# Recurrent two-tower kernel: output sizes folded into the combine weights, high part cast on VectorE, groups half a stage apart

## The chip, the cores and the metric

The kernel runs on one core of a Trainium2 chip. The metric is the device time of one execution in microseconds (us), the median of several runs. The engines named below are TensorE (PE in the profile; its weight loads are PEld), VectorE (DVE), ScalarE (ACT), GpSimd (POOL) and SyncE (SP, which here only issues transfers).

## What is computed

The reference scans 128 steps. At each step a batch of 512 rows with 12 features goes through two small residual towers, and the step's result `delta` replaces feature 3 of the next step. The path tower does not see `delta`; the flat tower does, so only the flat tower and the head form a chain from step to step.

```python
def _leaky(x):
    return jnp.where(x >= 0, x, NEG * x)          # NEG = 0.2
def _tower(x, w_in, b_in, blocks):
    h = _leaky(x @ w_in + b_in)
    for w1, b1, w2, b2 in blocks:                  # two blocks
        h = _leaky(_leaky(h @ w1 + b1) @ w2 + b2 + h)
    return h
def step(prev_delta, xk):
    fk, k = xk                                     # fk: 512 x 12
    d = jnp.where(k == 0, fk[:, DELTA_IDX], prev_delta)
    fk = fk.at[:, DELTA_IDX].set(d)                # DELTA_IDX = 3
    fe = _tower(fk[:, :4], fw_in, fb_in, flat_blocks)
    pe = _tower(fk[:, 4:], pw_in, pb_in, path_blocks)
    h = _leaky(jnp.concatenate([fe, pe], axis=-1) @ cw1 + cb1)
    delta = jax.nn.sigmoid(h @ cw2 + cb2)[:, 0]
    return (delta, delta)
```

All hidden widths are 128, all data float32.

## The kernel before

Hidden units lie on the 128 partitions and the batch on the columns. The flat tower and the head work on two **groups** of 256 columns (g = 0 and 1). The path tower works on all 512 columns, with its products split in two halves (h = 0 and 1). One **stage** is one step k of the scan; in the stage of step k the path tower works ahead, on steps k+1, k+2 and k+3.

**Products.** A float32 product (`product`, L438; `onto`, L441; `combine_path`, L528; `combine_flat`, L533) is one matmul call on 256 columns and shows as two matmul instructions in the profile. A stage has 20 of them: 8 of the path tower, 8 of the flat tower (`flat_1a`, `flat_1b`, `flat_2a`, `flat_2b` for two groups), 4 of the head's combine layer. Seven calls per stage work on split operands of the type fp32r and show as one instruction each: `path_in` (512 columns, L453), `flat_x` (256 columns, one per group, L497), `output_high` (L541) and `output_low` (L546), one each per group. For the last two the head activation is split into a high part rounded to fp32r (`head_hi`) and a remainder (`head_lo`). They multiply with `cw2_sign`, a matrix of +1 and -1, because the sizes |cw2| are already in the head activation: ScalarE computes leaky(|cw2|*x + |cw2|*cb1), with `cw2_size` as its scale and `cb1_scaled` as its bias.

**Order of work.** Each engine has a list of calls written by hand, `body(k)`, run for k = -3 to 127; an engine runs its own list strictly in order, and semaphores tie the lists together. So the place of a call in its engine's list decides when it can run at the earliest. Between the products of a group ScalarE computes an activation: `flat_1a` on TensorE, `flat_1a` on ScalarE (tile `f_mid`), `flat_1b` on TensorE, `flat_1b` on ScalarE (`f_res`), and the same again for block 2, then `combine_flat`, `head_out` and `head_high` on ScalarE, `head_low` on VectorE, the two output products, `delta_out` on ScalarE (sigmoid), then `flat_delta` and `flat_in` on VectorE (`f_t`, `f_in`) for the next step. VectorE also adds the residual input to the result bank ahead of the second product of a block (`flat_1b_old`, `flat_2b_old`), and makes the path tower's sums and results (`path_1b_sum`, `path_1b`, `path_2b_sum`, `path_2b`; tiles `p_sum`, `p_res`). ScalarE makes `p_in` and `p_mid`.

TensorE's list before is `body` at L549, ScalarE's at L300, VectorE's at L417.

**Set-up.** SyncE loads the features in four chunks; VectorE (chunk 0) and GpSimd (chunks 1 to 3) split them into a high and a low part, which are stored to memory and loaded again per step (`x_flat`, `x_path`). The weights `hidden_w` are one transfer. Before its list TensorE waits for the weights and for `cw2_sign` and `cb1_scaled` (`s_cw2`), and opens the two result banks with one product each.

## Time and profile before

| | |
|---|---|
| median of 3 runs | 1308.1 us (1307.48 to 1308.73) |
| profiled execution, its own time | 1308.0 us |
| span, first to last instruction of it | 1306.2 us |
| TensorE busy | 1284.5 us (98% of the span), 6020 matmuls |
| weight loads busy | 1049.5 us (80%) |
| VectorE busy | 866.4 us (66%) |
| ScalarE busy | 996.0 us (76%) |
| granted TensorE clock, mean | 0.997 of full speed |

Matmuls are pipelined: one starts before the one before it has ended, and their ends are modelled. A busy TensorE is therefore not one at its peak; the distance from one start to the next tells more than the busy share. In a stretch of the trace the start of a matmul that stood waiting is recorded when its weight load begins, and its columns flow somewhat later.

### The profile page before, as it was taken

What the parts mean: (1) busy time and instruction counts of PE and PEld (TensorE: products, weight loads), DVE (VectorE), ACT (ScalarE), POOL (GpSimd) and SP (SyncE); (2) the same over time, 40 slices, a digit from 0 to 9 for tenths busy, and PEclk for the clock granted to TensorE, in tenths of its full rate; (3) what the DMA queues carried; (4) which work ended last, traced back from release to release, by engine and by line L of the source; (5) the groups of instructions that cost most, each with busy time, mean ns of one, the idle gap of its engine ahead of it and who ended that gap; (6) DMA issues with size and microseconds to landing.
All of it is one profiled execution on the core that took longest, in us unless ns stands there. A gap on an engine that the chain in (4) does not pass through costs nothing.

```text
span 1306.2 us, 20302 instructions
## 1 busy us (share of the span) xinstructions
PE 1284.5 (98%) x6020; PEld 1049.5 (80%) x6020; DVE 866.4 (66%) x1801; ACT 996.0 (76%) x2177; POOL 23.2 (2%) x19
## 2 busy tenths in 40 slices
PE   5999999999999999999999999999999999999998
PEld 3788888888888888888888888888888888888885
DVE  4676666666666666666766666666676666666665
ACT  1677877777787777777778777777777777777786
POOL 6000000000000000000000000000000000000000
PEclk9999999999999999999999999999999999999999
DMA  4400000000000000000000000000000000000000
GB/s 151 190 10 9 11 11 9 9 12 10 9 11 11 9 11 10 10 9 11 11 9 11 11 9 10 11 10 9 11 10 10 11 10 10 10 11 10 9 7 2
DMA packets 14033, 23.53 MB, mean 18 GB/s; under 512 B 6324, under 2 KB 6760, under 8 KB 13160
## 3 DMA queue, kind: packets, MB, share of 16 engines
q1 hardware_dynamic: 13640, 22.23, 5.4%
q8 instruction: 53, 0.87, 0.3%
q14 instruction: 52, 0.43, 0.1%
q10 hardware_dynamic: 288, 0.01, 0.0%
HBM read 15.66 MB, written 6.55 MB: 17 GB/s over the span
## 4 chain that ended last, share of the span: by engine, by line
PE 97%; DVE 1%; ACT 1%; DMA 1%; issue 0%; SPq 0%; DVEq 0%; ACTq 0%
PE ps_path L438 34%; PE ps_res L441 19%; PE ps_flat L438 17%; PE ps_head L528 8%; PE ps_head L533 8%; PE ps_head L541 4%; PE ps_path L453 2%; PE ps_head L546 2%; PE ps_flat L497 2%; DVE p_res L347 1%; DMA x_lo<-chunk_lo 0%; ACT head L244 0%; DMA chunk_x<-x 0%; ACT head_hi L244 0%; DVE p_sum L350 0%
## 5 line engine op out<-in xcount | busy, mean ns | idle before, releaser
L244 ACT ACTIVATE f_mid<-ps_flat,columns_sb 128x256 f32<-128x256 f32 x512 | 243.0, 475 | 190.3 <-PE ps_flat L438 184.0
L441 PE MATMUL ps_res<-f_mid,hidden_w 128*128 128x256 f32 x1024 | 318.6, 393 | 0.5
L438 PE MATMUL ps_path<-p_mid,hidden_w 128*128 128x256 f32 x1024 | 306.4, 382 | 0.8 <-ACT p_mid L244 0.8
L244 ACT ACTIVATE f_res<-ps_res 128x256 f32<-128x256 f32 x512 | 196.1, 383 | 62.9 <-PE ps_res L441 62.6
L350 DVE SCALAR_TENSOR_TENSOR p_sum<-ps_path,columns_sb,p_res 128x512 f32<-128x512 f32 x128 | 96.0, 750 | 223.0 <-PE ps_path L438 223.0
L441 PEld LDWEIGHTS ps_res<-f_mid,hidden_w 128*128 128x128 f32 x1024 | 164.3, 188 | 82.6 <-ACT f_mid L244 43.2
L438 PEld LDWEIGHTS ps_path<-p_mid,hidden_w 128*128 128x128 f32 x1024 | 196.0, 192 | 28.6 <-ACT p_mid L244 1.5
L407 DVE TENSOR_SCALAR ps_res<-f_res,columns_sb 128x256 f32<-128x256 f32 x256 | 123.6, 483 | 121.0 <-ACT f_res L244 121.0
L347 DVE SCALAR_TENSOR_TENSOR p_res<-p_sum 128x512 f32<-128x512 f32 x256 | 182.3, 712 | 0.1
L244 ACT ACTIVATE p_mid<-ps_path,columns_sb 128x512 f32<-128x512 f32 x256 | 175.1, 684 | 7.7 <-PE ps_path L438 7.7
L528 PE MATMUL ps_head<-p_res,hidden_w 128*128 128x256 f32 x512 | 153.5, 382 | 3.8 <-DVE p_res L347 3.8
L438 PE MATMUL ps_flat<-f_in,hidden_w 128*128 128x256 f32 x512 | 153.4, 381 | 0.3 <-DVE f_in L347 0.2
L438 PE MATMUL ps_path<-p_in,hidden_w 128*128 128x256 f32 x512 | 151.9, 383 | 1.6 <-ACT p_in L244 1.5
L533 PE MATMUL ps_head<-f_res,hidden_w 128*128 128x256 f32 x512 | 152.4, 379 | 0.0
L438 PE MATMUL ps_flat<-f_res,hidden_w 128*128 128x256 f32 x512 | 152.4, 379 | 0.0
L414 DVE TENSOR_TENSOR head_lo<-head,head_hi 128x256 fp32r<-128x256 f32 x256 | 108.8, 425 | 65.1 <-ACT head_hi L244 65.1
L244 ACT ACTIVATE head<-ps_head,cb_scaled,cw_size 128x256 f32<-128x256 f32 x256 | 144.2, 563 | 6.4
L438 PE MATMUL ps_path<-p_res,hidden_w 128*128 128x256 f32 x512 | 148.3, 382 | 0.6 <-DVE p_sum L350 0.6
L244 ACT ACTIVATE head_hi<-ps_head,cb_scaled,cw_size 128x256 fp32r<-128x256 f32 x256 | 143.9, 562 | 0.0
L297 ACT ACTIVATE delta<-ps_head,cb_col 128x256 f32<-128x256 f32 x256 | 121.3, 474 | 24.3 <-PE ps_head L546 24.0
L385 DVE SCALAR_TENSOR_TENSOR f_t<-delta,columns_sb,ps_flat 128x256 f32<-128x256 f32 x256 | 121.1, 473 | 0.0
L546 PE MATMUL ps_head<-head_lo,cw_sign 128*128 128x256 f32 x256 | 119.6, 467 | 0.4
(39 smaller groups left out, 1390.0 us busy)
## 6 DMA issues: line engine op xcount, KB each, us to landing
x_path<-x_hi SPq DMA_DIRECT2D x256, 16.0 KB
x_path<-x_lo SPq DMA_DIRECT2D x256, 16.0 KB
x_flat<-x_hi SPq DMA_DIRECT2D x256, 6.0 KB
x_flat<-x_lo SPq DMA_DIRECT2D x256, 6.0 KB
chunk_x<-x SPq DMA_DIRECT2D x2, 1152.0 KB, 7.2
x_hi<-chunk_hi SPq DMA_DIRECT2D x2, 1152.0 KB, 8.8
x_lo<-chunk_lo SPq DMA_DIRECT2D x2, 1152.0 KB, 11.4
out<-delta SPq DMA_DIRECT2D x128, 2.0 KB
```

Of the source, the lines that this page charges most:

```text
L244: return act.activation(dst, src, ACT.Prelu, bias=bias, scale=scale, alpha=NEG)
L297: act.activation(cols(delta[par], g), outcome(g), ACT.Sigmoid, bias=cb2_col[:, :]).then_inc(s_delta[g], 1)
L347: return dve.scalar_tensor_tensor(dst, src, NEG, src, ALU.mult, ALU.max)
L350: return dve.scalar_tensor_tensor(dst, products, bias, old, ALU.add, ALU.add)
L385: dve.scalar_tensor_tensor(f_t[g][:, :], cols(delta[1 - par], g), column["delta_w"], second(ps_flat, g), ALU.mult, ALU.add).then_inc(s_f_i ...
L407: dve.tensor_scalar(layer(ps_res, g), f_res1[g][:, :], column["fr2_b2"], None, ALU.add).then_inc(s_f2b_old[g], 1)
L414: dve.tensor_tensor(head_lo[g][:, :], head[g][:, :], head_hi[g][:, :].bitcast(fp32), ALU.subtract).then_inc(s_head_lo[g], 1)
L438: return pe.matmul(dst, weight[w_name], src, start=True, stop=True)
L441: return pe.matmul(dst, weight[w_name], src, start=False, stop=True, skip_group_check=True)
L528: pe.matmul(combined(g), weight["cw1_path"], cols(p_res2[par], g), start=True, stop=False)
L533: pe.matmul(combined(g), weight["cw1_flat"], f_res2[g][:, :], start=False, stop=True)\
L546: pe.matmul(outcome(g), cw2_sign[:, :], head_lo[g][:, :], start=False, stop=True)\
```

## The change

1. **Sizes into the weights.** `cw1_flat` and `cw1_path` are multiplied once, at the start, by |cw2| of their output column (`cw1_scaled`). For that, cw2 is loaded as one row by a third transfer on ScalarE's queue, spread over the partitions by a product with a row of ones, and made positive on VectorE. The head activation keeps its bias `cb1_scaled` and loses its scale.
2. **High part on VectorE.** `head_high` is no longer a second activation of the bank on ScalarE but a VectorE copy of `head` to the type fp32r, ahead of `head_low`.
3. **`path_1b`** (leaky of `p_sum1`) moves from VectorE to ScalarE.
4. **New lists.** On all three engines group 1 now runs ahead of group 0: `flat_delta`, `flat_in` and `flat_1a` of group 1 for step k+1 stand at the end of the stage of step k. SyncE's list is the same (its calls only compute `par` themselves).

The diff, cut to its core:

```diff
@@ set-up
+        one_row, cw2_row = sb("one_row", [1, HID]), sb("cw2_row", [1, HID])
+        cw2_copy, cw2_sizes, cw1_scaled = sb("cw2_copy", [HID, HID]), sb("cw2_sizes", [HID, HID]), sb("cw1_scaled", [HID, 2 * HID])
+        cw2_rows = ps_res[0][:, 0:HID]
+            pool.memset(one_row[:, :], 1.0).then_inc(s_one_row, 1)
@@ block.scalar
+            act.dma_start(cw2_row[:, :], w["columns"][:, cw2_at:cw2_at + 1].rearrange("p a -> a p"),
+                          allow_slow_non_contiguous=True)\
+               .then_inc(s_columns, 16)
             act.preload_act_table(ACT.Sigmoid)
-            act.wait_ge(s_columns, 32)
-            act.wait_ge(s_cw2, 1)
+            act.wait_ge(s_columns, 48)
+            act.wait_ge(s_cw2, 4)
+            def path_1b(k):
+                par = k % 2
+                if exists(k):
+                    act.wait_ge(s_p1b_t, k + 1)
+                    leaky(p_res1[par][:, :], p_sum1[:, :]).then_inc(s_p1b_h, 1)
             def head_out(k, g):
...
-                    leaky(head[g][:, :], combined(g), cb1_scaled[:, :], cw2_size[:, :]).then_inc(s_head_h[g], 1)
-            def head_high(k, g):
-                if exists(k):
-                    act.wait_ge(s_head_mm[g], k + 1)
-                    leaky(head_hi[g][:, :], combined(g), cb1_scaled[:, :], cw2_size[:, :]).then_inc(s_head_hi[g], 1)
+                    leaky(head[g][:, :], combined(g), cb1_scaled[:, :]).then_inc(s_head_h[g], 1)
@@ list of ScalarE, new
+            def body(k):
+                flat_1a(k, 0)
+                flat_1b(k, 1)
+                flat_1b(k, 0)
+                flat_2a(k, 1)
+                flat_2a(k, 0)
+                flat_2b(k, 1)
+                path_1b(k + 2)
+                flat_2b(k, 0)
+                head_out(k, 1)
+                head_out(k, 0)
+                path_in(k + 3)
+                delta_out(k, 1)
+                path_2a(k + 2)
+                delta_out(k, 0)
+                path_1a(k + 3)
+                flat_1a(k + 1, 1)
@@ block.vector
+            dve.wait_ge(s_cw2_rows, 1)
+            dve.tensor_copy(cw2_copy[:, :], cw2_rows).then_inc(s_cw2_parts, 1)
+            dve.wait_ge(s_cw2_parts, 3)
+            dve.scalar_tensor_tensor(cw2_sizes[:, :], cw2_copy[:, :], -1.0, cw2_copy[:, :],
+                                     ALU.mult, ALU.max).then_inc(s_cw2_parts, 1)
+            dve.wait_ge(s_cw2_parts, 4)
+            dve.wait_ge(s_w_loaded, 16)
+            for i, n in enumerate(("cw1_flat", "cw1_path")):
+                dve.tensor_tensor(cw1_scaled[:, i * HID:(i + 1) * HID], weight[n], cw2_sizes[:, :],
+                                  ALU.mult).then_inc(s_cw2, 1)
+            def head_high(k, g):
+                if exists(k):
+                    dve.wait_ge(s_head_h[g], k + 1)
+                    dve.tensor_copy(head_hi[g][:, :], head[g][:, :]).then_inc(s_head_hi[g], 1)
@@ list of VectorE, new
+            def body(k):
+                flat_delta(k, 0)
+                flat_in(k, 0)
+                flat_1b_old(k, 1)
+                flat_1b_old(k, 0)
+                path_1b_sum(k + 2)
+                flat_2b_old(k, 1)
+                flat_2b_old(k, 0)
+                path_2b_sum(k + 1)
+                path_2b(k + 1)
+                head_high(k, 1)
+                head_low(k, 1)
+                head_high(k, 0)
+                head_low(k, 0)
+                flat_delta(k + 1, 1)
+                flat_in(k + 1, 1)
@@ list of TensorE, new
+            def body(k):
+                flat_1a(k, 0)
+                flat_1b(k, 1)
+                path_1b(k + 2, 1)
+                flat_1b(k, 0)
+                flat_2a(k, 1)
+                path_2b(k + 1, 1)
+                flat_2a(k, 0)
+                flat_2b(k, 1)
+                combine_path(k, 0)
+                flat_2b(k, 0)
+                combine_flat(k, 1)
+                flat_x(k + 1, 0)
+                path_in(k + 3)
+                combine_flat(k, 0)
+                flat_x(k + 1, 1)
+                path_2a(k + 2, 0)
+                output_high(k, 1)
+                path_2a(k + 2, 1)
+                output_low(k, 1)
+                output_high(k, 0)
+                path_1a(k + 3, 0)
+                output_low(k, 0)
+                path_1a(k + 3, 1)
+                combine_path(k + 1, 1)
+                path_2b(k + 2, 0)
+                flat_1a(k + 1, 1)
+                path_1b(k + 3, 0)
@@ TensorE, ahead of its list
+            pe.wait_ge(s_one_row, 1)
+            pe.wait_ge(s_columns, 48)
+            pe.matmul(cw2_rows, one_row[:, :], cw2_row[:, :], start=True, stop=True).then_inc(s_cw2_rows, 1)
-            pe.wait_ge(s_cw2, 2)
+            pe.wait_ge(s_cw2, 4)
+            pe.wait_ge(s_cw2_parts, 3)
             for g in range(GROUPS):
                 product(layer(ps_res, g), "fr1_w2", hidden_w[:, slice(*GROUP_COLS[g])]).then_inc(s_res_open[g], 1)
```

## Rows read from the trace of the kernel before

**Rows 1.** Waits, 300 to 1000 us: waiter, what it waited for, us, times, longest.

```profile
PEld ps_res L441 <- ACT f_mid L244: 22.6, 71, 0.3
```

**Rows 2.** Timeline of one stage, TensorE: start us, us, engine, line, out<-in, count.

```profile
602.18 0.59 PE L438 MATMUL ps_flat<-f_in,hidden_w 128*128 128x256 f32 x2
...
605.63 0.59 PE L438 MATMUL ps_flat<-f_res,hidden_w 128*128 128x256 f32 x2
...
607.33 0.59 PE L533 MATMUL ps_head<-f_res,hidden_w 128*128 128x256 f32 x2
...
608.19 0.59 PE L533 MATMUL ps_head<-f_res,hidden_w 128*128 128x256 f32 x2
...
608.74 0.59 PE L438 MATMUL ps_path<-p_in,hidden_w 128*128 128x256 f32 x2
...
609.32 0.59 PE L438 MATMUL ps_path<-p_in,hidden_w 128*128 128x256 f32 x2
...
610.23 0.60 PE L438 MATMUL ps_path<-p_res,hidden_w 128*128 128x256 f32 x2
...
612.08 0.38 PE L438 MATMUL ps_flat<-f_in,hidden_w 128*128 128x256 f32 x1
```

**Rows 3.** The same stage, ScalarE and weight loads; in brackets idle time before.

```profile
606.26 0.48 ACT L244 ACTIVATE f_mid<-ps_flat,columns_sb 128x256 f32<-128x256 f32 x1 [0.39 <-PE ps_flat L438]
...
606.79 0.30 PEld L441 LDWEIGHTS ps_res<-f_mid,hidden_w 128*128 128x128 f32 x2 [0.32 <-ACT f_mid L244]
...
608.87 0.56 ACT L244 ACTIVATE head<-ps_head,cb_scaled,cw_size 128x256 f32<-128x256 f32 x1
...
609.32 0.57 ACT L244 ACTIVATE head_hi<-ps_head,cb_scaled,cw_size 128x256 fp32r<-128x256 f32 x1
```

**Rows 4.** Groups by line, whole span: shapes xcount | busy us, mean ns | idle before.

```profile
L244 ACT ACTIVATE f_mid<-ps_flat,columns_sb 128x256 f32<-128x256 f32 x512 | 243.0, 475 | 190.3 <-PE ps_flat L438 184.0
L244 ACT ACTIVATE f_res<-ps_res 128x256 f32<-128x256 f32 x512 | 196.1, 383 | 62.9 <-PE ps_res L441 62.6
...
L244 ACT ACTIVATE head<-ps_head,cb_scaled,cw_size 128x256 f32<-128x256 f32 x256 | 144.2, 563 | 6.4
...
L414 DVE TENSOR_TENSOR head_lo<-head,head_hi 128x256 fp32r<-128x256 f32 x256 | 108.8, 425 | 65.1 <-ACT head_hi L244 65.1
...
L244 ACT ACTIVATE p_in<-ps_path 128x512 f32<-128x512 f32 x128 | 75.8, 592 | 15.4 <-PE ps_path L453 15.4
...
L343 DVE TENSOR_SCALAR cw_sign<-cw_twice 128x128 fp32r<-128x128 f32 x1 | 0.2, 221 | 0.0
...
L338 DVE SCALAR_TENSOR_TENSOR cw_size<-columns_sb 128x1 f32<-128x1 f32 x1 | 0.2, 158 | 0.0
```

**Rows 5.** Timeline of set-up and fill, all engines.

```profile
4.09 1.12 POOL L224 MEMSET x_path<- 64x512 f32 x2
4.21 0.55 DVE L330 CAST in_split<-in_raw 128x256 fp32r<-128x256 f32 x1
...
6.91 2.07 PE L438 MATMUL ps_res<-hidden_w 128*128 128x256 f32 x4 [6.91 <-DMA hidden_w<-hidden]
...
11.11 0.80 PE L453 MATMUL ps_path<-x_path,in_split 128*128 128x512 f32 x1 [2.13 <-DMA x_path<-x_lo]
...
28.09 5.37 POOL L231 TENSOR_TENSOR chunk_lo<-chunk_x,chunk_hi 128x2304 fp32r<-128x2304 f32 x1
...
29.25 4.76 DVE L347 SCALAR_TENSOR_TENSOR p_res<-p_sum 128x512 f32<-128x512 f32 x1
...
35.93 0.63 PE L438 MATMUL ps_flat<-f_in,hidden_w 128*128 128x256 f32 x1
```

**Rows 6.** Timeline of the end: first product of the last two stages, last sigmoid.

```profile
1285.59 0.70 PE L438 MATMUL ps_flat<-f_in,hidden_w 128*128 128x256 f32 x2
...
1295.41 0.70 PE L438 MATMUL ps_flat<-f_in,hidden_w 128*128 128x256 f32 x2 [0.15 <-DVE f_in L347]
...
1304.08 0.47 ACT L297 ACTIVATE delta<-ps_head,cb_col 128x256 f32<-128x256 f32 x1 [0.44 <-PE ps_head L546]
```

More of the change, by code:

```diff
@@ L198, in _ @@
             sp.wait_ge(s_chunk_stored[0], 32)
-            body(0, 0)
-            body(1, 1)
+            body(0)
+            body(1)
             for c in range(1, CHUNKS):
@@ L298, in delta_out @@
                                    bias=cb2_col[:, :]).then_inc(s_delta[g], 1)
-            def body(k, par):
+            def body(k):
                 flat_1a(k, 0)
-                flat_1a(k, 1)
+                flat_1b(k, 1)
                 flat_1b(k, 0)
-                flat_1b(k, 1)
+                flat_2a(k, 1)
                 flat_2a(k, 0)
-                flat_2a(k, 1)
+                flat_2b(k, 1)
+                path_1b(k + 2)
                 flat_2b(k, 0)
+                head_out(k, 1)
+                head_out(k, 0)
                 path_in(k + 3)
-                flat_2b(k, 1)
-                head_out(k, 0)
-                head_high(k, 0)
-                head_out(k, 1)
-                head_high(k, 1)
-                delta_out(k, par, 0)
+                delta_out(k, 1)
+                path_2a(k + 2)
+                delta_out(k, 0)
                 path_1a(k + 3)
-                delta_out(k, par, 1)
-                path_2a(k + 2)
+                flat_1a(k + 1, 1)
             bodies(act, body)
@@ L375, in path_2b, with flat_delta @@
                     leaky(p_res2[par][:, :], p_sum2[:, :]).then_inc(s_p2b_h, 1)
-            def flat_delta(k, par, g):
+            def flat_delta(k, g):
+                par = k % 2
                 if exists(k):
@@ L527, in combine_path @@
                         pe.wait_ge(s_delta[g], k)
-                    pe.matmul(combined(g), weight["cw1_path"], cols(p_res2[par], g), start=True, stop=False)
+                    pe.matmul(combined(g), cw1_path, cols(p_res2[par], g), start=True, stop=False)
             def combine_flat(k, g):
@@ L532, in combine_flat @@
                     pe.wait_ge(s_f2b_h[g], k + 1)
-                    pe.matmul(combined(g), weight["cw1_flat"], f_res2[g][:, :], start=False, stop=True)\
+                    pe.matmul(combined(g), cw1_flat, f_res2[g][:, :], start=False, stop=True)\
                       .then_inc(s_head_mm[g], 1)
@@ L547, in output_low, with body @@
                       .then_inc(s_out_mm[g], 1)
-            def body(k, par):
+            def body(k):
                 flat_1a(k, 0)
-                combine_path(k, par, 1)
-                flat_1a(k, 1)
+                flat_1b(k, 1)
+                path_1b(k + 2, 1)
                 flat_1b(k, 0)
-                path_1b(k + 2, 1)
-                flat_1b(k, 1)
+                flat_2a(k, 1)
+                path_2b(k + 1, 1)
                 flat_2a(k, 0)
-                path_2b(k + 1, 0)
-                flat_2a(k, 1)
+                flat_2b(k, 1)
+                combine_path(k, 0)
                 flat_2b(k, 0)
-                path_in(k + 3, 1 - par)
-                flat_2b(k, 1)
+                combine_flat(k, 1)
+                flat_x(k + 1, 0)
+                path_in(k + 3)
                 combine_flat(k, 0)
-                path_2b(k + 1, 1)
-                combine_flat(k, 1)
-                flat_x(k + 1, 1 - par, 1)
+                flat_x(k + 1, 1)
[4 more added lines that the diff above has]
+                output_high(k, 0)
                 path_1a(k + 3, 0)
-                output_high(k, 0)
+                output_low(k, 0)
                 path_1a(k + 3, 1)
-                output_low(k, 0)
-                flat_x(k + 1, 1 - par, 0)
-                output_high(k, 1)
-                path_2a(k + 2, par, 0)
-                output_low(k, 1)
-                path_2a(k + 2, par, 1)
-                combine_path(k + 1, 1 - par, 0)
+                combine_path(k + 1, 1)
+                path_2b(k + 2, 0)
+                flat_1a(k + 1, 1)
                 path_1b(k + 3, 0)
```

72 lines of the change are left out of this document (34 added, 38 removed).

## The prediction

> **What bounds the kernel now.** The table of the profile says that TensorE is busy for 98% of the span, but that share is modelled, so I read it last. First I read the waits of the steady part: one wait of TensorE stands there once per stage, the weight load of a `ps_res` product for ScalarE's `f_mid`, 22.6 us over 71 stages, 0.32 us each [rows 1]. Then I read the starts of TensorE's matmuls over one stage [rows 2]. From the first `flat_1a` at 602.18 to the next at 612.08 is 9.90 us, the length of a stage. Eight products lie between 602.18 and 605.63, so a float32 product that waits for nothing takes F = 0.431. Between 608.19 and 608.74 lie one product and one `flat_x`: a split product of 256 columns takes r = 0.55 - 0.43 = 0.12. `path_in` never stands alone there; it streams 512 columns like one of the two passes of a float32 product, so I estimate R = 0.22 (half of F). A stage without any wait would be 20 x 0.431 + 6 x 0.12 + 0.22 = 9.56. So 0.34 of the 9.90 is lost, and the starts say where [rows 2]: 605.63 to 607.33 holds three products and `path_in` (1.51) but takes 1.70, lost 0.19; 608.74 to 609.32 holds a product and `output_high` (0.55) but takes 0.58, lost 0.03; 609.32 to 610.23 holds a product and three split ones (0.79) but takes 0.91, lost 0.12. That is all of it. The kernel is bound by TensorE's work, and only 0.34 us per stage is to be had by order.
>
> The three losses have causes. **Hand-over by way of ScalarE:** the `flat_2a` product that starts at 605.63 lets its activation start at 606.26, 0.63 later; that ends 0.48 later, at 606.74; the weight load starts at 606.79 [rows 2, 3], and its product streams from 607.33 - 0.43 = 606.90, 0.16 after the end. So from one product of a block to the next a group needs 0.63 + 0.475 + 0.16 = 1.265, while TensorE's list puts only two products and `path_in` in between, 1.08: the 0.19. The other two losses are `output_high` waiting for ScalarE's second activation `head_hi`: it ends at 609.32 + 0.57 = 609.89 [rows 3], and the product streams from 610.23 - 0.12 = 610.11, 0.22 after it (this call waits for two semaphores).
>
> **The change, part by part.** I laid TensorE's new list out with the same F, r and R, from `flat_1a(k,0)` at 0: `flat_1b(1)` 0.43, `flat_1b(0)` 1.29, `flat_2a(1)` 1.72, `flat_2a(0)` 2.59, `flat_2b(1)` 3.02, `flat_2b(0)` 3.88, `combine_flat(1)` 4.31, `path_in` 4.86, `combine_flat(0)` 5.08, `output_high(1)` 6.06, `output_low(1)` 6.61, `output_high(0)` 6.73, `path_1a` 6.85, `output_low(0)` 7.28, `flat_1a(k+1,1)` 8.70, end 9.56. The work on TensorE is the same: 20 products and 7 split ones. Now each hand-over is held against it.
> - Before a `1b` or `2b` product every group now has three products between: 1.293, needed 1.265 [rows 2 to 4]. The 0.19 is gone, 0.03 to spare. From `flat_1b` to `flat_2a` and `flat_2b(1)` to `combine_flat(1)` 0.63 + 0.383 + 0.16 = 1.17 is needed in 1.293; from `flat_2b(0)` to `combine_flat(0)` in 2F + r + R = 1.20, again 0.03 to spare [rows 2, 4].
> - Head activation: `f_mid` with one operand per partition takes 475 ns, `head` with two 563 [rows 4]. Without the scale it costs 0.475. The second activation (0.56 of ScalarE twice a stage) goes.
> - High part on VectorE, cost d. No steady row shows a cast. A VectorE operation with one input from the same memory took 221 ns on 128 columns with output fp32r, and one on a single column 158 [rows 4]: half a nanosecond per column, so d = 0.158 + 0.13 = 0.29 on 256. The other end is the one cast of just this shape, 0.55 [rows 5], which ran while GpSimd was filling tiles; `head_lo`, with two inputs, takes 0.425 [rows 4]. I take 0.29, as GpSimd has no work after 28.09 + 5.37 = 33.5 [rows 5]. Behind the casts, which wait for ScalarE's `head`, VectorE has queued `head_low` and `flat_delta(k+1,1)`; the latter waits for a later sigmoid anyway.
> - `output_high(0)`, the tightest place: from `combine_flat(0)` the list leaves 3F + 3r = 1.65. Needed are 0.63 + 0.475 + 0.03 + 0.29 + 0.22 = 1.65 [rows 2 to 4]; zero to spare, so I put 0.02 of stall here. `path_1a(k+3,0)` right behind it needs 0.63, the head's slot on ScalarE, `p_in` 0.592 [rows 4] and 0.16. The slot is less than the duration: `head` at 608.87 takes 0.563 and the next starts 0.45 later, an overlap of 0.11 [rows 3, 4]; so 0.37, at worst the whole 0.475. That gives 1.75 to 1.86 against 1.77: covered by the same 0.02, at worst 0.09.
> - `path_1b` on ScalarE: like `p_in`, 0.592 [rows 4], at worst the 0.68 of an activation with a bias. It waits for the path sum, whose product streams at 0.86 and which is done before 2.5, and it stands ahead of the activation of `flat_2b(0)`. Its gap there is from 3.02 + 0.63 + 0.28 = 3.93 to 3.88 + 0.63 = 4.51: 0.58, and with the overlap of 0.11 it fills 0.48 of it. Cost nothing; if it took 0.68 without overlap, 0.07 per stage before `combine_flat(0)`. VectorE is rid of it: an operation on 512 columns by the slope of `head_lo`, some 0.7 [rows 4].
> - `path_2a` now stands ahead of `delta_out(k,0)` on ScalarE, which is pushed from 7.6 to 7.9. Behind it: sigmoid 0.475, two VectorE operations of 0.43 to 0.47, hand-overs 0.03, 0.03, 0.16: `flat_1a(k+1,0)` could stream at 9.48, wanted at 9.56. Nothing, with 0.08 to spare.
> So the stage becomes 9.56 + 0.02 = 9.58, 0.32 less than 9.90; over 125 full stages 40.0 us.
> - **Fill.** The path tower's result on VectorE stood for 4.76 us at 29.25, until GpSimd's subtraction, begun at 28.09, had ended; undisturbed it would take the 0.7 above. First `flat_1a` was at 35.93 [rows 5]. Now `path_1b` is on ScalarE, so this result comes earlier, but `flat_in` of step 0, the same kind of VectorE operation, meets the same subtraction and ends near 33.8; group 0 follows 1.0 later: 34.9. A gain of 1.0 (0 to 1.5).
> - **Set-up.** The row product, the copy and four more VectorE operations start when the weights land at 6.91 and take some 2.2 us (product 0.8, the rest 0.16 to 0.3 each [rows 4]); then the two opening products take their 2.07. `path_in` started at 11.11, when its data came [rows 5]: 6.91 + 2.2 + 2.07 = 11.2, cost 0.1. Were the scattered load of the row late, TensorE would stand with it: up to 3 us. The third transfer is issued ahead of ScalarE's table load and GpSimd's extra fill ahead of the tiles' fills; both engines are idle for a while before 11.11, so neither costs.
> - **End.** The last stages have no path work, so the group's own chain sets their length: four block hand-overs 4.9, head to low product 2.1, sigmoid to next `flat_1a` 1.9, in all 8.9, say 9.1 with queueing, against 1295.41 - 1285.59 = 9.82. And the last sigmoid started 1304.08 - 1295.41 = 8.67 after the last `flat_1a(0)` [rows 6]; by the chain (4.9 + 2.1, and 0.3 to the sigmoid) it would be 7.3. Two such stages and the end: 1.4 + 1.3 = 2.7; I take 2.4 (1.5 to 3).
>
> Sum: 40.0 + 1.0 - 0.1 + 2.4 = 43.3 off the profiled execution's 1308.0 (span 1306.2 and 1.8 around it): 1264.7. The median of the runs is 1308.1, so 1264.8, and I say 1265.
>
> **The cast, rule against row.** The trace's only cast of 128x256 took 0.55 [rows 5], and by that row the change loses. The Trainium skill, VectorE: DVE Perf Modes, The perf-mode tier table, says that an fp32 `tensor_copy` within SBUF runs at twice the rate of a `tensor_tensor` (1227 against 2293 ns at 2048 columns); by an estimate from it the cast takes 0.29, and the time is the forecast's. The Trainium skill, GPSIMD Engine Reference, Specifications, adds that this engine shares its SBUF interfaces with VectorE instructions of that two-port kind; by that rule 0.55 is a disturbed value, and the row agrees, as a GpSimd fill from 4.09 to 5.21 covers the cast.
>
> **The rivals.**
> 1. *Hand-overs without slack.* Six hand-overs keep 0 to 0.03. If the new neighbours make each some 0.03 to 0.05 longer, they add up to 0.1 to 0.2 per stage: gain 0.22 to 0.12 x 125, plus the ends 3.3: 1277 to 1290. For it: the sum is made from rows rounded to 0.01. Against: from `flat_1a` to `flat_1b` the old list has the same three products between, and TensorE lost nothing there (eight products in a row without loss [rows 2]).
> 2. *The cast without double rate*, 0.425 like `head_lo` [rows 4]. VectorE's queue of `head_high(1)`, `head_low(1)`, `head_high(0)` then ends last: `output_high(0)` streams at 4.31 + 0.63 + 0.475 + 0.03 + d + 0.10 + 0.34 + d + 0.22 = 6.11 + 2d, wanted at 6.73; the stall is 2d - 0.62 = 0.23. Stage 9.79, gain 0.11 x 125 + 3.3 = 17: 1291.
> 3. *Slower: the cast as slow as its one row.* With d = 0.55 the same queue gives 0.48, stage 10.04: 125 x 0.14 - 3.3 = 14 more, 1322. It decides from d = 0.50 on, where the stall eats the 0.34 and the ends. For it: the one row of this shape. Against: no GpSimd work beside it after 33.5, and the 221 ns row.
> 4. *No gain:* the wait of rows 1 comes back at another place at its full size, for instance in the loop of group 0, which has 0.08 to spare: 1304 to 1309.
>
> **How the numbers follow.** Forecast 0.67 (own range 1261 to 1272: stage 9.56 to 9.62, ends 1.5 to 4.5), rival 1 0.17, rival 2 0.06, rival 3 0.07, rival 4 0.03. The range 1261 to 1285 holds the forecast and most of rival 1, about 0.8. A difference of 0.2% (2.6 us) is about what can be told from none. Faster 0.67 + 0.17 + 0.06 = 0.90, same 0.03, slower 0.07.
>
> **What would show it.** The wait of rows 1 gone; `flat_1a(k,0)` 9.58 apart; casts of 0.28 to 0.30; `head` at 0.475; ScalarE's `p_res` near 0.6; TensorE's only small gap ahead of `output_high(0)`; first `flat_1a(0)` near 35; from the last one to the last sigmoid about 7.4. Wrong would make it a cast above 0.35, a gap ahead of `combine_flat(0)` (activations that don't overlap), or TensorE's loads of two neighbouring split products (`output_low(1)`, `output_high(0)`) taking over 0.12 each.

## The result, and the profile after

The changed kernel takes 1265.07 us (median of 4 runs, 1264.49 to 1265.59) where the kernel before takes 1307.79 beside it on the same chip (4 runs, 1307.29 to 1308.73). The ratio is 0.9672, with a 95% interval of 0.9656 to 0.9689: 3.3% faster. The forecast was 1265.0. The profiled execution took 1264.49 us, its span is 1262.7, and the mean granted clock of TensorE is 0.999 against 0.997 before.

The busy shares come last in weight, as before: TensorE's is 98% in both kernels (1243.4 us busy after the change), though one of them is 43 us shorter.

What matters are the waits between 300 and 1000 us (waiter, what it waited for, total us, times, longest). The wait of [rows 1], 22.6 us over 71 stages, has shrunk to this:

```profile
PEld ps_res L469 <- ACT f_mid L257: 0.2, 1, 0.2
```

No other wait of TensorE is listed there. Before, a second one stood once per stage beside that of [rows 1], at the weight load of `output_high`, which the prediction found by the starts alone:

```profile
PEld ps_head L541 <- issue: 11.5, 71, 0.2
```

("issue" names no releaser; this call waits for two semaphores.) The stage of [rows 2] now reads so (start us, us, engine, line, operation, out<-in; TensorE's matmuls alone):

```profile
602.25 0.59 PE L466 MATMUL ps_flat<-f_in,hidden_w 128*128 128x256 f32 x2
...
606.56 0.59 PE L567 MATMUL ps_head<-f_res,cw_scaled 128*128 128x256 f32 x2
...
607.11 0.40 PE L484 MATMUL ps_path<-x_path,in_split 128*128 128x512 f32 x1
607.35 0.59 PE L567 MATMUL ps_head<-f_res,cw_scaled 128*128 128x256 f32 x2
...
608.45 0.59 PE L466 MATMUL ps_path<-p_res,hidden_w 128*128 128x256 f32 x2
...
609.00 0.29 PE L575 MATMUL ps_head<-head_hi,cw_sign 128*128 128x256 f32 x1
609.12 0.59 PE L466 MATMUL ps_path<-p_in,hidden_w 128*128 128x256 f32 x2
...
611.83 0.59 PE L466 MATMUL ps_flat<-f_in,hidden_w 128*128 128x256 f32 x2
```

From `flat_1a(k,0)` at 602.25 to the next at 611.83 is 9.58 us; before it was 9.90 (9.907 as the mean between 300 and 1000 us). Eleven products start 0.43 apart from 602.25 to 606.56, through the place where the old list lost 0.19.

Each activation and cast that the change touches, as groups by line ([rows 4] has before's; shapes, count, total us, mean ns, idle before them):

```profile
L257 ACT ACTIVATE head<-ps_head,cb_scaled 128x256 f32<-128x256 f32 x256 | 121.3, 474 | 45.4 <-PE ps_head L567 39.4
L257 ACT ACTIVATE p_res<-p_sum 128x512 f32<-128x512 f32 x128 | 79.6, 622 | 5.1 <-DVE p_sum L374 5.1
...
L435 DVE CAST head_hi<-head 128x256 fp32r<-128x256 f32 x256 | 75.3, 294 | 136.2 <-ACT head L257 136.2
```

The set-up and the fill, answering to [rows 5] (timeline, several engines; in brackets idle time before and what ended it):

```profile
4.23 1.14 POOL L233 MEMSET x_path<- 64x512 f32 x2
...
4.62 0.29 DVE L344 CAST in_split<-in_raw 128x256 fp32r<-128x256 f32 x1 [0.19 <-DMA in_raw<-inputs]
...
6.99 0.79 PE L617 MATMUL ps_res<-cw_row,one_row 1*128 1x128 f32 x2 [6.99 <-DMA hidden_w<-hidden]
...
9.23 2.08 PE L466 MATMUL ps_res<-hidden_w 128*128 128x256 f32 x4 [1.44 <-DVE cw_sign L367]
...
11.29 0.80 PE L484 MATMUL ps_path<-x_path,in_split 128*128 128x512 f32 x1
...
28.07 5.37 POOL L240 TENSOR_TENSOR chunk_lo<-chunk_x,chunk_hi 128x2304 fp32r<-128x2304 f32 x1
...
28.96 4.75 DVE L371 SCALAR_TENSOR_TENSOR f_in<-f_t 128x256 f32<-128x256 f32 x1
...
34.95 1.06 PE L466 MATMUL ps_flat<-f_in,hidden_w 128*128 128x256 f32 x2
```

`f_in` waits out the subtraction on GpSimd: it should take 0.43 and takes 4.75, until 33.71, 0.27 after GpSimd's end at 33.44. TensorE stood idle for 4.05 us ahead of the product at 33.77, and soon after it its granted clock fell to the lower of its two levels, 0.50 of full speed (1.2 of 2.4 GHz):

```profile
34.50:37.00 2.50, 2.50 (x7) 0.50 0.00 0
```

(stretch, its length, TensorE busy, matmuls, granted clock, DMA.) It was at 1.00 again from 38.0. At the lower level products start 0.86 apart (34.95, 35.81, 36.66), so this stage takes 11.06 us, from 34.95 to 46.01. Before, the first stage took 11.40, from 35.93 to 47.33, and the granted clock was 0.50 from 33 to 38. The prediction has nothing on the clock.

The end, answering to [rows 6], with the first product of stages 125 and 126 and the last sigmoid:

```profile
1234.54 0.59 PE L466 MATMUL ps_flat<-f_in,hidden_w 128*128 128x256 f32 x2
...
1243.90 0.70 PE L466 MATMUL ps_flat<-f_in,hidden_w 128*128 128x256 f32 x2 [0.21 <-DVE f_in L371]
...
1253.82 0.47 ACT L257 ACTIVATE f_mid<-ps_flat,columns_sb 128x256 f32<-128x256 f32 x1 [0.38 <-PE ps_flat L466]
...
1260.62 0.47 ACT L312 ACTIVATE delta<-ps_head,cb_col 128x256 f32<-128x256 f32 x1 [0.27 <-PE ps_head L580]
```

Cut at the first `flat_1a(0)` and at that of stage 125, the two spans compare so (before's 1275.84 is the same product in its timeline):

| part | before | after | difference | forecast |
|---|---|---|---|---|
| until the first `flat_1a(0)` | 35.93 | 34.95 | -1.0 | -0.9 (fill -1.0, set-up +0.1) |
| 125 stages | 1239.9 | 1199.6 | -40.3 | -40.0 |
| from there to the end | 30.4 | 28.2 | -2.2 | -2.4 |

### The profile page after: what moved, and what is told of

It reads as the page before. It is cut to its first block, busy times and chain, and to the rows that moved or that the text cites. A ratio compares the mean times of both kernels' runs of the same rounds, so it can differ in the third digit from the quotient of the medians.

```text
span 1262.7 us, 20315 instructions
## 1 busy us (share of the span) xinstructions
PE 1243.4 (98%) x6022; PEld 1062.1 (84%) x6022; DVE 888.8 (70%) x1933; ACT 931.3 (74%) x2049; POOL 23.0 (2%) x20
## 4 chain that ended last, share of the span: by engine, by line
PE 98%; DVE 1%; ACT 0%; issue 0%; DMA 0%; SPq 0%; DVEq 0%; ACTq 0%
PE ps_path L466 35%; PE ps_flat L466 18%; PE ps_res L469 18%; PE ps_head L567 9%; PE ps_head L562 9%; PE ps_path L484 2%; PE ps_head L580 2%; PE ps_head L575 2%; PE ps_flat L530 2%; DVE f_in L371 0%; DMA hidden_w<-hidden 0%; DVE p_sum L374 0%; PE ps_res L466 0%; DVE f_t L407 0%; SPq L201 0%
## 5 line engine op out<-in xcount | busy, mean ns | idle before, releaser
L469 PE MATMUL ps_res<-f_mid,hidden_w 128*128 128x256 f32 x1024 | 305.6, 380 | 0.2
L466 PEld LDWEIGHTS ps_path<-p_mid,hidden_w 128*128 128x128 f32 x1024 | 191.4, 191 | 33.2 <-ACT p_mid L257 2.4
L469 PEld LDWEIGHTS ps_res<-f_mid,hidden_w 128*128 128x128 f32 x1024 | 168.7, 189 | 54.1 <-ACT f_mid L257 1.7
L374 DVE SCALAR_TENSOR_TENSOR p_sum<-ps_path,columns_sb,p_in 128x512 f32<-128x512 f32 x128 | 96.1, 751 | 137.1 <-PE ps_path L466 137.1
L435 DVE CAST head_hi<-head 128x256 fp32r<-128x256 f32 x256 | 75.3, 294 | 136.2 <-ACT head L257 136.2
L257 ACT ACTIVATE head<-ps_head,cb_scaled 128x256 f32<-128x256 f32 x256 | 121.3, 474 | 45.4 <-PE ps_head L567 39.4
L562 PE MATMUL ps_head<-p_res,cw_scaled 128*128 128x256 f32 x512 | 152.4, 379 | 0.1
L567 PE MATMUL ps_head<-f_res,cw_scaled 128*128 128x256 f32 x512 | 152.3, 379 | 0.0
L530 PE MATMUL ps_flat<-x_flat,in_split 128*128 128x256 f32 x256 | 119.5, 467 | 0.0
L371 DVE SCALAR_TENSOR_TENSOR f_in<-f_t 128x256 f32<-128x256 f32 x256 | 113.1, 442 | 8.9
```

What stands on the lines that cost most here:

```text
L257: return act.activation(dst, src, ACT.Prelu, bias=bias, alpha=NEG)
L371: return dve.scalar_tensor_tensor(dst, src, NEG, src, ALU.mult, ALU.max)
L374: return dve.scalar_tensor_tensor(dst, products, bias, old, ALU.add, ALU.add)
L466: return pe.matmul(dst, weight[w_name], src, start=True, stop=True)
L469: return pe.matmul(dst, weight[w_name], src, start=False, stop=True, skip_group_check=True)
L530: pe.matmul(second(ps_flat, g), flat_in_w, cols(x_flat[par], g), start=True, stop=True)\
```

## The experiments

The theory is the sum of the prediction: TensorE's work fixes 9.56 us per stage, and what is above that is a hand-over that is longer than the products put in between. Its rivals: the operations alone, or the order alone, bring the gain; the slack of the hand-overs isn't where the sum has it; the 0.55 us cast of [rows 5] is a price that the cast can have in this kernel too. Every time below stands beside runs of the kernel before on the same chip (medians 1308.3, 1308.5 and 1308.6 for the three chips). "Period" is the time between two `flat_1a(k,0)`, one near 300 us and one near 1000, divided by the stages between.

**The order alone.** The new lists, with the old operations in them: `head_high` on ScalarE with the scale, `path_1b` on VectorE.

```diff
@@ list of ScalarE, against the changed kernel
                 flat_2b(k, 1)
-                path_1b(k + 2)
                 flat_2b(k, 0)
                 head_out(k, 1)
+                head_high(k, 1)
                 head_out(k, 0)
+                head_high(k, 0)
@@ list of VectorE
                 flat_2b_old(k, 1)
                 flat_2b_old(k, 0)
+                path_1b(k + 2)
                 path_2b_sum(k + 1)
                 path_2b(k + 1)
-                head_high(k, 1)
                 head_low(k, 1)
-                head_high(k, 0)
                 head_low(k, 0)
```

> The new lists with the old operations: high part a second activation on ScalarE, scale in the activation, path_1b on VectorE. Theory (order and offload need each other): ScalarE's queue head 1, high 1, head 0, high 0, p_in is too long for the new places; the high part of group 0 ends near 6.86 after the stage's start, p_in near 7.34, so output_high(0) is 0.35 late and path_1a(k+3,0) 0.65 late: stage 10.2, time near 1344 us. Rival (the order alone removed the wait before flat_2b(1) and does most of the gain): about 1270 to 1285 us.

Measured: 1347.86 us, ratio 1.0301 (1.0284 to 1.0318), period 10.234. It is slower than before by 40 us. Its waits between 300 and 1000 us, and the place in the timeline:

```profile
PEld ps_head L586 <- issue: 34.4, 137, 0.3
...
PEld ps_path L477 <- ACT p_in L257: 16.5, 69, 0.2
```

```profile
606.73 0.57 ACT L257 ACTIVATE head_hi<-ps_head,cb_scaled,cw_size 128x256 fp32r<-128x256 f32 x1
...
607.18 0.61 ACT L257 ACTIVATE p_in<-ps_path 128x512 f32<-128x512 f32 x1
...
607.83 0.30 PEld L477 LDWEIGHTS ps_path<-p_in,hidden_w 128*128 128x128 f32 x2 [0.24 <-ACT p_in L257]
```

Four head activations now stand in a row on ScalarE (they start at 605.36, 605.83, 606.28 and 606.73), and `p_in` comes behind them: `path_1a` waits 0.24 for it, and the weight load of `output_high`, which needs `head_hi`, waits 34.4 / 137 = 0.25 for each group. So the new order alone removes the wait of [rows 1] and puts larger ones in its place.

**The operations alone.** The lists of before, with the new operations.

```diff
@@ list of VectorE, against the changed kernel
...
+                head_high(k, 0)
+                head_low(k, 0)
                 path_2b_sum(k + 1)
-                path_2b(k + 1)
                 head_high(k, 1)
                 head_low(k, 1)
-                head_high(k, 0)
-                head_low(k, 0)
-                flat_delta(k + 1, 1)
-                flat_in(k + 1, 1)
+                path_2b(k + 1)
@@ list of TensorE
...
                 flat_2a(k, 1)
+                flat_2b(k, 0)
+                path_in(k + 3)
+                flat_2b(k, 1)
+                combine_flat(k, 0)
                 path_2b(k + 1, 1)
...
```

> The old lists with the new operations: sizes in the weights, cast on VectorE, path_1b on ScalarE right after head_out of group 0. Theory: the 0.19 before flat_2b(1) stays, and VectorE's queue head_high 0, head_low 0, path_2b_sum, head_high 1 makes output_high(1) 0.4 late: stage 10.1, time near 1337 us. Rival (the offload of ScalarE is what pays): 0.15 of the 0.34 comes back, stage 9.75, 1290 us.

Measured: 1341.77 us, ratio 1.0253 (1.0237 to 1.0268), period 10.18. The waits, and VectorE's list at the high part:

```profile
PEld ps_head L575 <- issue: 24.2, 68, 0.5
PEld ps_res L469 <- ACT f_mid L257: 22.5, 71, 0.3
PE ps_head L575 <- DVE head_hi L435: 12.3, 68, 0.3
```

```profile
602.33 0.74 DVE L374 SCALAR_TENSOR_TENSOR p_sum<-ps_path,columns_sb,p_res 128x512 f32<-128x512 f32 x1
...
602.99 0.28 DVE L435 CAST head_hi<-head 128x256 fp32r<-128x256 f32 x1
...
603.39 0.19 PEld L575 LDWEIGHTS ps_head<-head_hi,cw_sign 128*128 128x128 f32 x1 [0.35 <-issue]
```

The wait of [rows 1] stands unchanged (22.5 us, 71 times), for it comes from the order. And the cast, 0.28 long, starts only when a path sum of 0.74 has left VectorE, so `output_high(1)`, which comes second in this order, waits, 0.35 at its weight load here. TensorE's starts give the loss: from the product at 602.41 to that at 603.61 lie one product and three split ones (0.79), and they take 1.20, lost 0.41. Each half alone costs 34 to 40 us; together they save 43.

**How long the cast may be.** Two kernels with the same values in `head_hi`: the high part as an operation with two inputs, and the cast with a second one (into a tile that nobody reads) ahead of it.

```diff
-                    dve.tensor_copy(head_hi[g][:, :], head[g][:, :]).then_inc(s_head_hi[g], 1)
+                    dve.tensor_tensor(head_hi[g][:, :], head[g][:, :], head[g][:, :], ALU.max).then_inc(s_head_hi[g], 1)
```

> The changed kernel with the high part made by an operation with two inputs (maximum of head with itself), 0.425 instead of 0.29. Theory (rival 2 of the prediction, stall 2d - 0.62 at output_high(0)): 0.23 of stall, stage 9.80, 1292 us. Rival (the cast is hidden, VectorE is idle a third of the time): 1265 us.

```diff
+                    dve.tensor_copy(spare[:, :], head[g][:, :])
                     dve.tensor_copy(head_hi[g][:, :], head[g][:, :]).then_inc(s_head_hi[g], 1)
```

> The changed kernel with every cast made twice, first into a spare tile. A cast's slot is 0.21, so d is 0.50, the point at which the prediction put the break-even with the kernel before: stall 0.38, stage 9.96, 1310 us. If the queue of casts is not what sets the end, the stall is that of one more slot alone (0.2 less the slack): 1290 us.

Measured: two inputs 1293.04 us, ratio 0.9881 (0.9866 to 0.9896), period 9.80; cast twice 1310.19 us, ratio 1.0012 (1.0003 to 1.0021), period 9.93. The operation with two inputs:

```profile
L435 DVE TENSOR_TENSOR head_hi<-head 128x256 fp32r<-128x256 f32 x256 | 108.2, 423 | 136.5 <-ACT head L257 136.5
```

With d = 0.423, 2d - 0.62 = 0.23, and 9.56 + 0.23 = 9.79 against 9.80. The cast alone grew by 0.13 and the stage by 0.22, so VectorE's queue of both groups' high parts sets the stall, as the formula of rivals 2 and 3 has it. In the other run the second cast starts 0.21 after the first and takes 0.29, so together they count as d = 0.50, the prediction's break-even:

```profile
609.97 0.29 DVE L436 CAST spare<-head 128x256 fp32r<-128x256 f32 x1 [1.05 <-ACT head L258]
610.18 0.29 DVE L437 CAST head_hi<-head 128x256 fp32r<-128x256 f32 x1
```

The stall by the formula is 0.38; measured are 9.93 - 9.56 = 0.37, and nothing of the gain is left (0.1% slower than before). Counted from the 9.58 to which the products of a stage add up as measured (next section) the two stalls are 0.22 and 0.35, so the formula holds within 0.03. The 43 us thus hang on one VectorE instruction, twice a stage, being 0.29 long and not 0.50.

**`path_1b` back on VectorE**, and nothing else.

```diff
@@ list of ScalarE
-                path_1b(k + 2)
@@ list of VectorE
                 flat_2b_old(k, 0)
+                path_1b(k + 2)
                 path_2b_sum(k + 1)
```

> The changed kernel with path_1b back on VectorE, between flat_2b_old(k,0) and path_2b_sum(k+1). Theory: in the steady part VectorE has room for it (done at 5.0, the first cast at 5.45), stage 9.58 as before; only the fill is later, since GpSimd holds this operation up: first flat_1a(0) 0 to 1 us later, 1265 to 1266 us. Rival (the move to ScalarE is needed): 0.2 or more per stage, 1290 us.

Measured: 1265.79 us, ratio 0.9674 (0.9661 to 0.9687), period 9.58. The changed kernel's ratio is 0.9672, so this part of the change is worth nothing that can be measured. VectorE held 0.7 us more work per stage without any loss. In the fill the first `flat_1a(0)` comes 1.5 later than in the changed kernel (36.42 against 34.95), as GpSimd's subtraction now holds up VectorE's path result again, but the second stage starts at 46.00 against 46.01: TensorE stood idle for 2.7 us ahead of the fill's last products and not for 4.05, its granted clock stayed at 1.00, and the first stage took 9.58 and not 11.06. This execution was the fastest of the five, 1263.86 with a mean granted clock of 1.000; three others had 0.997 and took 1265.8 to 1266.4. So the 2.5 us between its executions go with the granted clock.

**The scale kept.** The head activation gets back a scale operand per partition, filled with ones, so that the result doesn't change.

```diff
-                    leaky(head[g][:, :], combined(g), cb1_scaled[:, :]).then_inc(s_head_h[g], 1)
+                    leaky(head[g][:, :], combined(g), cb1_scaled[:, :], one_col[:, :]).then_inc(s_head_h[g], 1)
```

> The changed kernel with a scale operand (a column of ones) kept in the head activation, which then takes 0.563 instead of 0.475. Theory: output_high(0) has no slack, so the 0.09 shows almost fully: stall 0.08, stage 9.66, 1275 us. Rival (ScalarE is idle a quarter of the time and hides it): 1265 us.

Measured: 1276.63 us, ratio 0.9758 (0.9745 to 0.9771), period 9.68.

```profile
L258 ACT ACTIVATE head<-ps_head,cb_scaled,one_col 128x256 f32<-128x256 f32 x256 | 144.6, 565 | 34.2 <-PE ps_head L570 28.0
```

The activation is 0.09 longer, the stage 0.10: there was no slack on the way from `combine_flat(0)` to `output_high(0)`, as the sum had it. With the rest of the change in place, moving the sizes into the weights is worth some 11 us.

**`path_1b` on ScalarE made longer**, by a bias of zeros and a scale of ones.

```diff
-                    leaky(p_res1[par][:, :], p_sum1[:, :]).then_inc(s_p1b_h, 1)
+                    leaky(p_res1[par][:, :], p_sum1[:, :], zero_col[:, :], one_col[:, :]).then_inc(s_p1b_h, 1)
```

> The changed kernel with two operands per partition (ones and zeros) in ScalarE's path_1b: 0.80 instead of 0.62. Theory: its gap is 0.58 and its slot becomes 0.69, so the activation of flat_2b(0) starts 0.11 late and combine_flat(0), with 0.04 to spare, 0.07 late: stage 9.65, 1274 us. Rival (covered): 1265 us.

Measured: 1274.16 us, ratio 0.9738 (0.9725 to 0.9752), period 9.66. ScalarE at that place:

```profile
600.36 0.38 ACT L258 ACTIVATE f_res<-ps_res 128x256 f32<-128x256 f32 x1
600.64 0.80 ACT L258 ACTIVATE p_res<-p_sum,zero_col,one_col 128x512 f32<-128x512 f32 x1
601.34 0.37 ACT L258 ACTIVATE f_res<-ps_res 128x256 f32<-128x256 f32 x1
```

`p_res` sits between the two activations of `flat_2b`, 0.98 apart. It went from 0.622 to 0.804, by 0.18, and the stage from 9.58 to 9.66, by 0.08: 0.10 of slack was there. The prediction had 0.13: 0.10 of the gap of 0.58 unfilled, and 0.03 to spare before `combine_flat(0)`. The missing 0.03 is the duration, 0.622 where it took 0.592.

**GpSimd beside the casts.** From step 20 on, GpSimd does work of no use: 40 fills, then 40 copies of 128x512, each waiting for the one before.

```diff
+            pool.memset(busy_b[:, :], 1.0).then_inc(s_busy, 1)
...
+            pool.wait_ge(s_delta[0], 20)
+            for n in range(40):
+                pool.wait_ge(s_busy, n + 1)
+                pool.memset(busy_a[:, :], 0.0).then_inc(s_busy, 1)
+            for n in range(40, 80):
+                pool.wait_ge(s_busy, n + 1)
+                pool.tensor_copy(busy_a[:, :], busy_b[:, :]).then_inc(s_busy, 1)
```

> The changed kernel with 40 fills and then 40 copies of 128x512 tiles on GpSimd, each waiting for the one before, from step 20 on. It asks whether GpSimd work beside the cast makes it take the 0.55 us of its one row of before (rival 3). Theory (it does): in the stretch with fills or copies the cast is 0.1 to 0.6 longer than 0.294 and the stages of it are longer than 9.58, after it both are as before. Rival (the 0.55 had another cause): cast 0.29 throughout.

Measured: 1267.73 us in a single run, which is 3.2 above the changed kernel's profiled execution. The two stretches of GpSimd, and the cast's durations (ns, least, median, most) during the fills, during the copies, and after both:

```profile
227.40 23.52 POOL L249 MEMSET busy_a<- 128x512 f32 x40 [194.10 <-ACT delta L323]
250.99 29.59 POOL L252 COPY busy_a<-busy_b 128x512 f32<-128x512 f32 x40
```

```profile
L446 DVE CAST head_hi<-head x4: 289/384/706, 234.0 to 244.5; 128x256 fp32r<-128x256 f32 x4
...
L446 DVE CAST head_hi<-head x6: 294/546/699, 253.7 to 275.6; 128x256 fp32r<-128x256 f32 x6
...
L446 DVE CAST head_hi<-head x20: 293/294/295, 304.2 to 391.2; 128x256 fp32r<-128x256 f32 x20
```

Alone, the casts vary by 2 ns; beside GpSimd they reach 0.70 us. Three stages under the copies took 10.4 to 10.5 us each, two under the fills 9.7 and 10.0. The starts and durations say when a cast is lengthened. One pair of rows of this run:

```profile
254.71 0.68 POOL L252 COPY busy_a<-busy_b 128x512 f32<-128x512 f32 x1
254.84 0.70 DVE L446 CAST head_hi<-head 128x256 fp32r<-128x256 f32 x1
```

The copy ends at 255.39, the cast at 255.54. All six casts that were lengthened here, under fills and copies alike, end 0.14 to 0.15 after the GpSimd instruction beside them; the four of 289 to 294 ns met one that had 0.12 or less left to run. The 0.55 row of [rows 5] fits: the one fill running beside it

```profile
4.09 0.52 POOL L224 MEMSET x_path<- 64x512 f32 x1
```

ends at 4.61, the cast at 4.76. In the changed kernel the same cast starts at 4.62, when the running fill ends at 4.75, and takes 0.29. So 0.55 is what this engine's neighbour made of a cast of 0.29, and the forecast's choice between the two ends was sound because GpSimd is idle in the steady part.

**The fill's 4 us: GpSimd's subtraction in pieces.** The 28.96 + 4.75 row above suggests that the split of an input chunk on GpSimd costs the start some 4 us. First, pieces of 256 columns, all casts and then all subtractions, back to back:

```diff
+                pieces = [slice(a, min(a + PIECE, CHUNK_COLS[c])) for a in range(0, CHUNK_COLS[c], PIECE)]
+                for p in pieces:
+                    pool.tensor_copy(chunk_hi[c][:, p], chunk_x[c][:, p]).then_inc(s_chunk_hi[c], 1)
+                for n, p in enumerate(pieces):
+                    pool.wait_ge(s_chunk_hi[c], n + 1)
+                    pool.tensor_tensor(chunk_lo[c][:, p], chunk_x[c][:, p], chunk_hi[c][:, p].bitcast(fp32),
+                                       ALU.subtract).then_inc(s_chunk_split[c], 1)
```

> The changed kernel with GpSimd's cast and subtraction of chunks 1 to 3 in pieces of 256 columns. Theory: VectorE's flat_in of step 0 stands 4.75 us because the subtraction of 2304 columns is one instruction; between pieces VectorE gets its turn, so the first flat_1a starts near 30 instead of 33.8, and some VectorE operations of stage 0 wait up to 0.6 each: 1261 to 1263 us. Rival (VectorE stands until GpSimd is done with the chunk, however cut): no gain, 1265 us or 0.5 more.

Measured: 1271.10 us, ratio 0.9714 (0.9700 to 0.9727), period 9.58. Both expectations fell: it is 6 us slower than the changed kernel, and all of it lies in the fill.

```profile
26.71 12.57 DVE L375 SCALAR_TENSOR_TENSOR p_res<-p_sum 128x512 f32<-128x512 f32 x1
```

```profile
25.31 4.17 POOL L244 TENSOR_TENSOR chunk_lo<-chunk_x,chunk_hi 128x256 fp32r<-128x256 f32 x6
29.43 3.16 POOL L241 CAST chunk_hi<-chunk_x 128x256 fp32r<-128x256 f32 x9
32.56 6.17 POOL L244 TENSOR_TENSOR chunk_lo<-chunk_x,chunk_hi 128x256 fp32r<-128x256 f32 x9
```

An operation of 0.7 us on VectorE stood for 12.57 us, until 39.28, 0.55 after GpSimd's unbroken run of short instructions ended at 38.73. TensorE stood idle meanwhile, and its granted clock was 0.50 from 34 to 43. Shorter pieces gave VectorE no turn at all. The new theory: VectorE gets in only where GpSimd pauses between instructions. It says that the same pieces with a wait between each two would help, and that their size would matter little. Both were tried:

```diff
@@ GpSimd, against the changed kernel
+                for n, p in enumerate(pieces):
+                    if n:
+                        pool.wait_ge(s_chunk_split[c], n)
+                    pool.tensor_copy(chunk_hi[c][:, p], chunk_x[c][:, p]).then_inc(s_chunk_hi[c], 1)
+                    pool.wait_ge(s_chunk_hi[c], n + 1)
+                    pool.tensor_tensor(chunk_lo[c][:, p], chunk_x[c][:, p], chunk_hi[c][:, p].bitcast(fp32),
+                                       ALU.subtract).then_inc(s_chunk_split[c], 1)
```

> As e8_pieces, but every piece of GpSimd waits for the one before it, cast and subtraction in turn, so GpSimd's engine stands free for a moment between two pieces. Theory: VectorE gets its turn only in such a gap (in e8_pieces, where the pieces followed one another without one, its p_res stood 12.6 us). Then no VectorE operation stands longer than one piece, 0.7 us; the first flat_1a is near 30 and stage 0 is up to 2 us longer: 1261 to 1264 us. Rival (VectorE stands until GpSimd's list is empty): first flat_1a past 40, 1271 us or more.

> The same with pieces of 768 columns, three per large chunk. Theory: no VectorE operation stands longer than 1.9 us, GpSimd is done near 37 instead of 43: first flat_1a at 30 to 32, 1261 to 1264 us. Rival: as for e10_pieces_gap256, 1270 us.

Measured: 256 columns 1260.36 us, ratio 0.9622 (0.9602 to 0.9642); 768 columns 1259.54 us, ratio 0.9619 (0.9599 to 0.9638). Both beat the changed kernel (0.9672, and the intervals don't touch), and can't be told from each other. Both are a little below what was expected. With 256 columns (first fence) and 768 (second):

```profile
28.47 0.73 POOL L245 TENSOR_TENSOR chunk_lo<-chunk_x,chunk_hi 128x256 fp32r<-128x256 f32 x1
28.56 0.92 DVE L376 SCALAR_TENSOR_TENSOR f_in<-f_t 128x256 f32<-128x256 f32 x1
```

```profile
28.77 1.87 POOL L245 TENSOR_TENSOR chunk_lo<-chunk_x,chunk_hi 128x768 fp32r<-128x768 f32 x1
...
29.39 1.52 DVE L376 SCALAR_TENSOR_TENSOR f_in<-f_t 128x256 f32<-128x256 f32 x1
```

`f_in` now ends with the one piece that it met: 29.48 against 29.20, 30.91 against 30.64. The first `flat_1a(0)` starts at 30.16 and 30.97 instead of 34.95, the second stage at 40.37 and 40.82 instead of 46.01, and the steady stage is as before. So 4.8 and 4.0 us are won by the start and 5.6 and 5.2 by the second stage: TensorE no longer stands idle for 4 us, its granted clock is 1.00 from 28 to 40 (and its mean 1.000 in all nine executions, where the changed kernel has 0.997 to 0.999), and the first stage takes 10.2 and 9.9 instead of 11.06. These are the best versions here, 48 and 49 us below the kernel before. Against the first version in pieces they differ in two things, the wait and the order of casts and subtractions. The order was not run by itself, but there the run changed from subtractions to casts at 29.43 and back at 32.56, and neither change let VectorE in.

The Trainium skill, SBUF — State Buffer, Who interferes with whom, says that VectorE and GpSimd share a pair of ports under an exclusive lock, and that a VectorE instruction with two inputs in SBUF contends with a GpSimd instruction that reads SBUF. For one instruction the traces agree (`f_in` 4.75 beside the 5.37 us subtraction, 1.52 beside the 1.87 us piece); the 12.57 us over a run of 0.7 us pieces goes beyond the rule, and the measurement decides: the one that waits can be passed over from piece to piece. The set-up shows it too, where GpSimd's fills follow each other without a wait: the same cast of `in_split` takes 0.29 to 0.38 in most runs of the changed kernel and its variants, and 0.71, 0.72, 0.80 and 1.14 in four, where it ends 0.15 after the next fill or the one after that.

## Why the prediction was right, and where its terms were off

- **The bound and the ideal stage.** F = 0.431 and r = 0.12 stand in the new stage as in the old. R was an estimate of 0.22: from 606.56 to 607.35 lie one product, one `flat_x` and `path_in`, so it takes 0.79 - 0.431 - 0.12 = 0.24. That is 0.02 more per stage, 2.4 us in 125 stages, and the old stage held it too: it lost 0.32 and not 0.34.
- **`output_high(0)`.** For this tightest place a stall of 0.02 was put. It streams at 609.00 and `path_1a` at 609.12; between the products at 608.45 and 609.12 lie 0.67 where F + 2r = 0.671. The stall is 0.01 at most. The two errors of 0.02 cancel in the 9.58. That the stage came out to 0.01 us is luck: the total was right, its split between the two was not.
- **Activation and cast.** Forecast 0.475 and 0.29, measured 0.474 and 0.294. The step that bore the most weight, taking the cast's price from a row of another shape rather than from the one row of its own shape, held. Its slope is that of an operation with one input within SBUF, half that of `head_lo` (426 ns after). The Trainium skill, VectorE: DVE Perf Modes, The perf-mode tier table, gives such a copy twice the rate of the operation with two inputs; the runs with 294 and 423 ns agree once the fixed part of 158 ns is taken off (136 against 265).
- **The reason for the 0.55 row** held: the fill beside it. It was put loosely, as any fill from 4.09 to 5.21. What counts is the single fill that runs when the cast starts: the row's cast ends 0.15 after it, and the changed kernel's cast, with fills beside it too (4.23 to 5.37), met one with 0.14 left and took 0.29.
- **Slack.** The path to `output_high(0)`: none (0.09 longer, 0.10 lost), as summed. For `path_1b` on ScalarE 0.13 was summed and 0.10 measured, as the activation itself was 0.622 and not `p_in`'s 0.592 (it reads SBUF, `p_in` reads PSUM). That the move frees VectorE was right and without use: with it undone the time is the same.
- **The fill** gained 1.0 up to the first `flat_1a(0)`, as forecast and by the mechanism forecast: `f_in` ended at 33.71, "near 33.8". But the sum has nothing on the granted clock, which was 0.50 from 34.5 to 37.9 us here, and that counts for more than this term: in the profile with `path_1b` back on VectorE the first `flat_1a(0)` came 0.5 later than before, the clock did not fall, and the second stage started where it did in the changed kernel. That the 1.0 stands in the total is in part luck.
- **Set-up** cost 0.18 (`path_in` at 11.29 instead of 11.11) where 0.1 was forecast: from 6.99 to the opening products at 9.23 is 2.24, as summed (2.2), but the weights landed 0.08 later, and so the whole chain. The input of `path_in` landed at the same moment (its weight load shows 0.71 idle until the transfer `x_path<-x_lo`), so the trace can't tell which of the two the product waited for last.
- **The end** gained 2.2 where 2.4 was taken. The last `flat_1a(0)` starts at 1253.08, so stages 125 and 126 took 1243.90 - 1234.54 = 9.36 and 9.18, where 9.1 was taken, and before the first of them took 9.75 and not 9.82. TensorE's list for stage 125 still holds path products, which the prediction left out. From the last start to the end are 9.6 us, before 10.8: 1.2 gained where 1.3 was taken. The last sigmoid starts 7.54 after it, or 7.43 counted from the stream (its activation at 1253.82, less 0.63); the 8.67 of before was a start of the first kind and the chain's 7.3 a time of the second.
- **The rivals.** Hand-overs did not grow with new neighbours. The formula of rivals 2 and 3 was right within 0.03 and their premise, a longer cast, wrong: the two runs with d = 0.42 and a doubled cast put it to the test. Rival 4's place, the loop of group 0, shows no wait.

What remains argued: that the high part's place accounts for most of the loss in the order-alone run. By subtraction it is the 82.8 us between that run and the changed kernel, less some 11 for the scale and nothing for `path_1b`; it was not run by itself, and the parts need not add up, since in that run the scale lengthens four activations in a row.

## What to carry to other kernels

Where one engine's work is the bound, write its list out with start times from rows of the trace, and hold each hand-over by another engine against the work put in between: that gave each term of the stage here to 0.02 us. A new order and lighter operations may each lose alone and win together, so test neither half as a verdict on the other; and find the one term without slack, since all that is added there is paid in full, while 0.7 us elsewhere is free. An idle stretch of the engine that is the bound can cost more than itself: look at the granted clock behind it. Before a steady-state price is taken from a start-up row, look at what the neighbouring engines do beside it.

## What the runs showed of the hardware beyond that

- A VectorE operation with both inputs in SBUF stood for 12.57 us beside an unbroken run of 256-column instructions on GpSimd, though each of these took 0.35 to 0.7 us (one run). With a wait on a semaphore between them, VectorE waited for one piece only, at `f_in`: 0.92 us instead of 0.43 beside pieces of 0.73, 1.52 beside one of 1.87.
- GpSimd work stretches VectorE's cast even when it only fills a tile: the cast ends 0.15 us after the GpSimd instruction that ran when it started, or that started 0.03 after it (up to 706 ns from 294), and is untouched where that one has 0.14 or less left.
- TensorE's granted clock fell to 0.50 from 34.5 to 37.9 us, after it had stood idle for 4.05 us ahead of 33.77; it stayed at 1.00 in the profile with `path_1b` back on VectorE, where the last idle stretch was 2.7 us, but fell in other executions of that kernel (mean 0.997). At 0.50 products start 0.86 us apart instead of 0.43.
- ScalarE's activations behind each other overlap by 0.1 us, also where they differ in length: with `p_res` at 0.80, the next started 0.70 after it.
